# Load order in the head, two short orders on VectorE, and the place of the last value tile, in a pre-norm attention and feed-forward layer

## The reference, cut to what matters

```
x = x + attn(layernorm(x), Wqkv, bqkv, Wo, bo)
    # q, k, v = x @ Wqkv + bqkv;  softmax(q k^T / 16) v @ Wo + bo
x = x + ffn(layernorm(x))
    # h  = relu(x @ up_w)**2;          shared = h @ down_w
    # lat = (x @ fc1_w) @ expert_w * sum(top2(x @ gate_w));  routed = lat @ fc2_w
    # layernorm(shared + routed) * gamma + beta
```

## Time and profile before

| | us |
|---|---|
| median of three runs | 2366.54 (2366.09 to 2366.83) |
| the profiled execution's own time | 2362.46 |
| its span | 2360.7 |
| TensorE busy in it | 2309.0 (98%) |
| VectorE, GpSimd, ScalarE busy | 1773.2, 1571.0, 906.2 |

### The profile page before, as it was taken

The page is one execution under the profiler, slowest core; times in us unless marked ns, Lnnn a source line. Parts: engine busy times, 40 slices in busy tenths (PEclk is TensorE's granted clock), DMA queues, the critical chain, the costliest instruction groups (busy, mean ns, idle before and its releaser), DMA issues.

```text
span 2360.7 us, 31308 instructions
## 1 busy us (share of the span) xinstructions
PE 2309.0 (98%) x11224; PEld 1926.0 (82%) x11224; DVE 1773.2 (75%) x2945; ACT 906.2 (38%) x1706; POOL 1571.0 (67%) x1173
## 2 busy tenths in 40 slices
PE   8999999999999999999999999999999999999998
PEld 6888888888888788878887887887888788887786
DVE  6999958878878644855689865479795557989968
ACT  4322233333333343444433443442244443244452
POOL 4557626664666776599668479847749974866762
PEclk9999999999999999999999999999999999999999
DMA  9999746778778633443345345335434533543342
GB/s 251 302 302 286 257 143 200 202 230 299 205 209 234 212 105 93 134 126 116 99 125 173 107 128 127 116 94 159 151 103 126 136 107 111 184 147 130 90 141 87
DMA packets 215802, 386.48 MB, mean 164 GB/s; under 512 B 19552, under 2 KB 95456, under 8 KB 215008
## 3 DMA queue, kind: packets, MB, share of 16 engines
q1 hardware_dynamic: 214496, 382.38, 54.9%
q10 hardware_dynamic: 1152, 2.10, 0.2%
HBM read 260.67 MB, written 90.18 MB: 149 GB/s over the span
## 4 chain that ended last, share of the span: by engine, by line
PE 50%; DVE 21%; POOL 15%; DMA 6%; issue 5%; SPq 2%; ACT 1%; DVEq 0%; POOLq 0%; ACTq 0%
PE ps L2164 17%; PE ps L2166 16%; PE ps L2165 16%; POOL hq L2024 5%; DVE pturn L1315 5%; DMA pland<-pturn 4%; POOL wr1l L1940 2%; POOL wr2l L1940 2%; POOL wr0l L1940 2%; SPq L638 2%; DVE mx L1298 1%; DVE x L1342 1%; DVE hq L1495 1%; DMA stf<-ups 1%; DVE xi L1251 1%
## 5 line engine op out<-in xcount | busy, mean ns | idle before, releaser
L1940 POOL TENSOR_TENSOR wr1l<-stf,wr1h 128x512 fp32r<-128x512 f32 x183 | 262.0, 1432 | 141.0 <-ACT wr1h L967 140.9
L1940 POOL TENSOR_TENSOR wr0l<-stf,wr0h 128x512 fp32r<-128x512 f32 x184 | 261.1, 1419 | 141.3 <-ACT wr0h L967 141.0
L1940 POOL TENSOR_TENSOR wr2l<-stf,wr2h 128x512 fp32r<-128x512 f32 x183 | 260.1, 1421 | 136.0 <-ACT wr2h L967 135.6
L967 ACT CAST wr0h<-stf 128x512 fp32r<-128x512 f32 x184 | 114.5, 622 | 303.6 <-PE ps L2166 250.6
L967 ACT CAST wr1h<-stf 128x512 fp32r<-128x512 f32 x183 | 113.8, 622 | 300.7 <-PE ps L2166 248.8
L967 ACT CAST wr2h<-stf 128x512 fp32r<-128x512 f32 x183 | 113.9, 622 | 287.0 <-PE ps L2166 246.3
L1940 POOL TENSOR_TENSOR pt<-pland,pt 128x512 fp32r<-128x512 f32 x120 | 153.1, 1311 | 77.3 <-ACT pt L945 77.3
L935 ACT ACTIVATE prob<-ps,nm 128x512 f32<-128x512 f32 x128 | 86.4, 688 | 244.4 <-DVE nm L1306 244.4
L1315 DVE STREAM_TRANSPOSE pturn<-prob 128x512 f32<-128x512 f32 x128 | 131.8, 1094 | 60.1 <-DMA pland<-pturn 57.5
L1189 DVE TENSOR_TENSOR hr2l<-hq,hr2h 128x512 fp32r<-128x512 f32 x78 | 98.3, 1260 | 89.2 <-ACT hr2h L986 89.1
L1189 DVE TENSOR_TENSOR hr1l<-hq,hr1h 128x512 fp32r<-128x512 f32 x78 | 98.0, 1257 | 85.6 <-ACT hr1h L986 85.5
(11 more groups left out here) (478 smaller groups left out, 7761.0 us busy)
## 6 DMA issues: line engine op xcount, KB each, us to landing
stf<-ups SPq DMA_DIRECT2D x160, 256.0 KB, 3.2
stf<-downs SPq DMA_DIRECT2D x160, 256.0 KB, 2.9
pland<-pturn SPq DMA_DIRECT2D x120, 256.0 KB, 4.7
stf<-in_upw_dram SPq DMA_DIRECT2D x120, 256.0 KB, 2.7
stf<-in_down_dram SPq DMA_DIRECT2D x88, 256.0 KB, 2.6
x<-in_x_dram SPq DMA_DIRECT2D x32, 512.0 KB, 6.8
x1d<-x SPq DMA_DIRECT2D x32, 512.0 KB, 5.8
xi<-in_x_dram SPq DMA_DIRECT2D x28, 512.0 KB, 9.5
```

The source lines that it names most:

```text
L967: eng.copy(hi, src).then_inc(*a_w.up(K))
L1940: eng.tensor_tensor(lo, src, hi.bitcast(F32), ALU.subtract).then_inc(*done)
```

## The change

Five things move; no arithmetic is added or taken away.

- SyncE issues the loads of `("et", 2)` and `("f2", 2, 0)` (256 KB each) between the first and the second half of the first 512 rows, instead of behind the second half.
- The low half of `("et", 3)` goes from VectorE to GpSimd, where it stands behind the wait for `v_rst` and ahead of `("f2", 3)`. VectorE normalises seven groups instead of five, ScalarE nine instead of eleven.
- In chunks 0 to 6, behind value tile 1, VectorE makes the low half of slab 0 of the next chunk ahead of the transposes of slabs 2 and 3, instead of behind them.
- In chunks 1 to 7 VectorE's `prep` of j = 0 and 1 is done at j = 2.
- In chunk 7 the scores of block 2 come ahead of value tile 3 on TensorE; VectorE's maxima of block 2 come ahead of that tile's low half; ScalarE's exponentials of block 2 come ahead of that tile's high half, and with it ahead of the split of the shuffled blocks 0 and 1.

```diff
-        STG_DVE = [("et", 0), ("f2", 0, 0), ("f2", 0, 1), ("f2", 1, 1), ("f2", 2, 1), ("et", 3)]
+        STG_DVE = [("et", 0), ("f2", 0, 0), ("f2", 0, 1), ("f2", 1, 1), ("f2", 2, 1)]
-        NORM_DVE = (3, 6, 9, 12, 15)
+        NORM_DVE = (1, 3, 6, 9, 11, 13, 15)
...
             eng.dma_start(quad[:, :], quad_c).then_inc(*d_cst.up(0))
+            for k in STG[6:8]:
+                load_stage(k)
             load_cut(XI[0], d_xi[0], 0, xf, 8, 16)
...
-            for k in STG[6:15]:
+            for k in STG[8:15]:
...
+                    if c == 7 and t == 3:
+                        exps(2)
                     hi, _, src = v_parts(c, t)
...
-                    exps(even)
+                    if C > 1:
+                        exps(even)
                     pt_hi(even - 1)
...
-            low(stg_parts(("et", 3)), a_stg["et", 3], v_stg.up(("et", 3)))
             norm1(0, NORM_DVE)
...
-                    prep(c, j)
+                    if c and j == 2:
+                        for early in range(2):
+                            prep(c, early)
+                    if c == 0 or j >= 2:
+                        prep(c, j)
...
                 for t in range(4):
+                    if c == 7 and t == 3:
+                        maxima(2)
                     low(v_parts(c, t), a_v[c, t], v_v.up((c, t)))
+                    if c < 7 and t == 1:
+                        slab_low(c + 1, 0)
                     if c < 7 and t < 2:
                         turn1(c + 1, 2 * t)
                         turn1(c + 1, 2 * t + 1)
-                    if c < 7 and t == 1:
-                        slab_low(c + 1, 0)
...
-            maxima(2)
             for u in (1, 3):
                 pt_low(0, u)
...
-            for k in (("f2", 3), ("w", 1, 0)):
+            for k in (("et", 3), ("f2", 3), ("w", 1, 0)):
                 stage_low(k)
...
-                    if c == 7 and t <= 1:
+                    if c == 7 and t < 3:
                         for u in range(4):
                             s_unit(t, u)
...
-                    scores(even)
-                    if C >= 2:
+                    if C > 1:
+                        scores(even)
                         outputs(C - 2)
                     scores(odd)
```

More of the change, by code:

```diff
@@ L357, in layer @@
         g_chain = Chain(sem("g_chain"))
-        g_stg = ev("g_stg", [k for k in STG if k not in STG_DVE])
+        g_stg = ev("g_stg", sorted([k for k in STG if k not in STG_DVE],
+                                   key=lambda k: STG.index(k) - 2 * (k == ("et", 3))))
         g_slab = ev("g_slab", [k for k in SLABS if k not in SLAB_DVE])
@@ L1626, in _, with maxima, turns @@
             turn1(0, 3)
+            def maxima(g):
+                for kb in range(4):
+                    row_max(g, kb)
+                neg_max(g)
+            def turns(g):
+                for kb in range(4):
+                    turn_p(g, kb)
+                sums(g)
             for c in range(8):
@@ L1692, in _ @@
                     if c == 7 and t <= 1:
[L1693 to L1709, removed]
+                        maxima(t)
+                        turns(t)
             def residuals(C):
```

## The result

| | before | changed |
|---|---|---|
| median, same chip | 2365.78 us, 10 runs | 2371.55 us, 10 runs |
| profiled execution, own time | 2362.46 us | 2377.53 us |
| its span | 2360.7 us | 2375.4 us |

The ratio is 1.0027, 95% interval 1.0017 to 1.0038: 6.4 us slower (4 to 9), 5.8 by the medians. Run again beside other executions of the kernel before, the unedited changed kernel gave 1.0031 (1.0019 to 1.0043). The profiled execution is the slowest of its ten, so I read it together with the second one (`after_again`, 2367.0 of span).

What follows compares the result with a forecast made beforehand. VectorE, taking turns with GpSimd, was taken to set the pace in chunks and attention, not TensorE. Head +3.2, chunks -1.1, transition +2.4 gave +4.5 on 2366.5, so 2371.0 us; 8 in 10 for 2361.5 to 2374.5.

Steps and rivals of the forecast that it cites:

- the alternation: Head and transition: with both engines ready, each VectorE instruction of this kind waits for a whole one of GpSimd.
- figures for the chunks: Chunk edits: -0.7 at chunk 1, +0.2 at 4, nothing at 6, -0.4 at 7, given as -1.1 us in sum.
- VectorE wins the port often enough: Rival: norm and block 2's transposes not late, little but the head's loads counts, 2365.4 to 2367; 0 to +3 had 0.22.
- Transition, +2.4: Chunks to attention: low halves fall together and alternate, block 2's transposes start at 344.7 instead of 342.19, +2.4 us.
- Loads, +0.95: Head: rows' second half lands 1.3 us later, 0.35 comes back, so the reciprocal root is 0.95 late.
- Rest of the head, +2.25: Low half on GpSimd, seven groups: first transpose at 38.05; with the loads TensorE starts 1.6 late, slabs 0.7 and 0.85 more.
- chunk 1, -0.7: Head of chunk 1: the low half, issued behind transposes though its input was ready, goes first and saves 0.7 us.
- Chunks 2 to 7, -0.4: Later statistics waits in chunks 3 and 5 repaid at next boundaries: +0.2 at chunk 4, nothing at 6, -0.4 at 7.
- VectorE is the bound in the chunks: Chunks: VectorE, busy 36.42 of 37.00 us between two first-slab low halves, sets that stretch, not TensorE.
- TensorE's waits are what counts: Rival: first-slab (2.8), later statistics (2.0) and exponentials' (2.0) waits go, 2359.7; -3 to -8 had chance 0.12.

Runs made afterwards that it cites:

- after_again: The changed kernel, unedited, run and profiled a second time: 1.0031 against the kernel before.
- e4_transition: Kernel before with only block 2's scores, maxima and exponentials moved ahead of the last value tile: 1.0009, +2.1 us.
- e5_early_split: e4_transition with ScalarE's split of block 0 ahead of block 2's exponentials, and VectorE's two low halves of block 0 behind block 2's maxima: 1.0002.
- e1_loads: Kernel before with only SyncE's two weight loads moved ahead of the rows' second half: 1.0011, +2.6 us.
- e3_chunk: Kernel before with only the chunk edits, the next first slab's low half ahead of two transposes and `prep` deferred: 0.9992, -1.9 us.
- e6_selective: Kernel before with `prep` deferred and the first slab's low half ahead of the transposes only for chunks 1, 4, 6 and 7: 0.9968, -7.6 us.
- e2_low_norm: Kernel before with the fourth `et` weight's low half on GpSimd and seven norm groups on VectorE instead of five: 1.0017, +4.0 us.

## Why the prediction was right, and where it was not

The forecast was +4.5 and 2371.0; measured are +5.8 (and +5.3 by the medians of the second comparison) and 2371.55. The four parts alone sum to 2.6 + 4.0 - 1.9 + 2.1 = +6.8, each uncertain by about 2. The mechanism that carries the forecast, the alternation, was right. That the sum came so near is in part luck: two of its terms came out too low by 0.4 and 1 or more, two others too high by 0.3 and 0.4. The text's own figures for the chunks (-0.7, +0.2, 0 and -0.4) also add up to -0.9, not to -1.1.

- **The alternation** was the right rule. Forecast: first transpose 10.2 behind the root, block 2's transposes +2.5. Measured: 9.7 behind `nb`, and +1.96, twice in the changed kernel and once alone (`e4_transition`). The rival that VectorE wins the port often enough falls.
- **Transition, +2.4:** right in size (1.96). One link was missing. The text let ScalarE's split of block 0 stand behind the exponentials by the program's order alone; `e5_early_split` shows that the value tile holds it.
- **Loads, +0.95:** undersized. I took the rate of the moved pieces, 1.3; the landing came 1.65 later in two profiles and 3.0 in one. I also let 0.35 come back from `f2l`; 0.2 did. The root was 1.4 late in the first two.
- **Rest of the head, +2.25, and chunk 1, -0.7:** together +1.55 forecast, about +1.2 measured in stretch (b) (47.4 against a mean of 46.2), less than (b) scatters by itself. The forecast had TensorE wait 0.65 for the first slab, beyond the loads. It didn't: the slab's low half was done 11.8 behind `nb` in both profiles, and TensorE came only at 12.0 and 12.2, since part of its own work ran at half clock (mean granted clock 0.90 and 0.89). Where the clock was full from `nb` on (`e1_loads`, 10.97), the same slab would have been 0.8 late, by subtraction of these two. The slabs behind it cost 1.4 together (from chunk 0's to chunk 1's first matmul 35.23; 33.79 in `e3_chunk`): 0.4 at slab 2 and 0.7 at slab 3 where 0.7 and 0.85 were forecast, the rest mostly at slab 1.
- **Chunks 2 to 7, -0.4:** the failed step. Measured in (c) are +0.6 and +2.0 against the kernel before, +1.0 and +2.5 against the mean of the eight profiles with its chunks. The text put 1.5 of wait in chunk 3 and 0.9 in chunk 5, and said that part was absorbed "because the weight sums that followed sat out GpSimd anyway". In chunk 3 TensorE waited 0.74 in place of 0.67, not 1.5. In chunk 5 the sums sat out GpSimd more than before, the wait was 2.5, and the half clock took 1.7 to 2.7 more. On the other side chunks 3, 4 and 6 got shorter by 2.6 together (35.57, 34.08 and 36.67 before, 34.81, 33.82 and 35.05 now), where I had 0.2 lost and 0.4 gained.
- **"VectorE is the bound in the chunks":** wrong, and it was my first argument. The 36.42 busy of 37.00 holds the time in which VectorE stands at the port behind GpSimd. `e6_selective` takes no work from it and saves about 4 us up to the scores by order alone (two reorderings, the low half's and `prep`'s). For these waits the rival "TensorE's waits are what counts" was right at four boundaries of seven.

## What to carry to other kernels

Where two engines share a port, an engine's busy time is no measure of its work: look for the same instruction at its short duration, and count how many instructions of the other stand beside it. Splitting work over both can make the first one later (6.46 us for half the low halves, 4.91 for all); freeing a third engine that feeds the other may do so too, which is argued here and not shown alone. Count port turns, not work. When a reordering removes equal waits at several places, look at each place for whether the operand is there: here an edit at four boundaries saved 7.6 us (4.5 to 10.6), and the same edit at all seven 1.9 (between a loss of 0.5 and a gain of 4).

## What the hardware showed

- A pause of TensorE that ended at full clock may be followed by half clock: 2.56, 2.46 and 2.42 us of waiting in chunk 5 each were followed by 0.50 granted. But 3.0 us before the scores of block 3 in `e5_early_split`, 1.98 at that place in the kernel before, and 1.4 in its chunk 6 were not: the granted clock stayed at 1.00. The length alone doesn't decide.
- The transfers of the first 20 us differ by execution: with the same loads the rows' first half was in VectorE's hands at 13.3 to 15.1 us, the second at 18.4 to 21.1. A single profile can't price a move of loads to less than 1 us.
- Open: why `e2_low_norm` cost 4.0 by its times and about 1 by its trace, and what made the landing of the second half 8.40 once.
